# A transformer block in fp32: another order of work in the attention loop, at its beginning and end, and ScalarE issuing the last V stores of the first stage

## The chip, the cores and the metric

One core of a Trainium2 chip runs the whole kernel in one launch. The metric is the device time in microseconds. Three runs of the kernel before took 1292.84, 1295.64 and 1298.81 us; the median is 1295.64 us. The engines are TensorE (PE in the profile; PEld are its weight loads), VectorE (DVE), ScalarE (ACT), GpSimd (POOL) and SyncE (SP), which issues DMAs.

## The reference

The input `x` is 32 sequences of 100 rows with 320 features; the context has 361 rows of 192 features for each sequence. There are 20 heads of 16 features.

```
def _attn(x, ctx, wq, wk, wv, wo, bo, heads):
    q, k, v = x @ wq, ctx @ wk, ctx @ wv          # each split into heads
    sim = einsum('bhid,bhjd->bhij', q, k) * dh ** (-0.5)
    out = einsum('bhij,bhjd->bhid', softmax(sim, axis=-1), v)
    return out (heads joined) @ wo + bo
h1 = _ln(x, n1_g, n1_b)
x = _attn(h1, h1, q1, k1, v1, o1_w, o1_b, heads) + x
h2 = _ln(x, n2_g, n2_b)
x = _attn(h2, context, q2, k2, v2, o2_w, o2_b, heads) + x
h3 = _ln(x, n3_g, n3_b)
a, g = split(h3 @ ff_w1 + ff_b1, 2, axis=-1)
return (a * gelu(g)) @ ff_w2 + ff_b2 + x
```

## The kernel before

The program has three stages, each a block of its own in which every engine runs a list of instructions written out by hand; a block begins when all engines have left the one before it. Engines wait for each other by semaphores.

The first stage normalises `x` and computes queries, keys and values of the first ("own") attention for all 32 sequences, four at a time (eight groups `k`). ScalarE copies each sequence's values out of PSUM into `v_rows` (`copy_values`, L2295), and SP stores queries and keys (`qk_dram`, L1905) and values (`store_values`, L1860) to HBM.

The second stage is the attention phase. It works on one sequence in each of four roles at a time: in period `p` of the loop (`PERIODS`, 29 of them) `x = p` is in its second ("cross") attention, `s = p + 1` has its cross scores' maxima taken, `c = p + 2` is in its own attention and gets its cross queries and keys, and `f = p + 3` has its own maxima taken. `lead_in` fills this pipeline and `run_out` drains it. Each engine has its own `lead_in`, `period` and `run_out`, in which the calls stand in the order in which the engine does them. The names of the steps on TensorE: `self_scores(f, i)` (L168) is one half of the own scores, whose maximum VectorE takes (L175); `cross_scores(s, i)` (L786) is a pair of heads of the cross scores, ten calls for a sequence, each followed by VectorE's maximum (L1096) before the next may overwrite PSUM; `scores_for_exp(a, b, g, jt)` (L812) computes the scores again with the maximum in an extra row, for ScalarE's exponential (L1419), a = 1 for own, 2 for cross; there are two PSUM banks for it and 11 buffers for the exponentials. `times_v(a, b, g)` (L834) multiplies them with the values. `project_kc` (KC, L733 to L737) and `project_vc` (VC, L748 to L752) make cross keys and values from the context, `project_q2` and `turn_q2` (Q2, QT) the cross queries, `turn_max` (MT1, MT2; L797) turns the maxima, `turn_normalised` (T2) the normalised rows, `project_out` (O1, O2; L703, L706) is the output projection. These projections share three PSUM banks in turn, in the order of the lists `FILL_WORK`, `work_jobs` and `DRAIN_WORK`; a job waits for the bank of the job three before it.

SP moves operands between the steps. `load_qkv1(b)` brings the own queries, keys and values ("own stack", L86 to L103, nine loads); its first use of a stored sequence waits for all stores of the first stage. `load_context(b)` brings a context (L145, L146) as soon as GpSimd has split the one before it into high and low parts (`split_first`, `split_last`, L1656, L1657). `place_kc`, `place_q2` and `place_max` copy keys (L550), queries (L568) and maxima (L160) into the stacks that the scores read; `place_q2` waits until GpSimd has cleared the stack (`clear_cross`), `load_qkv1` likewise for `clear_own` (both L1610). SP works in order, so a step that waits holds up everything behind it.

The third stage is the feed-forward part, in five passes of 640 rows.

Of the kernel before, what the change touches and what calls it, by code (L numbers as in the profile page):

```python
# [31 lines left out]
NB = 4  # L32
# [12 lines left out]
def work_jobs(x, s, c, f):  # L45
    y = None if x is None or x == 0 else x - 1
    order = [("MT2", x, 0), ("VC", s, 2), ("O2", y, 0), ("MT1", f, 0), ("KC", c, 0), ("KC", c, 1), ("O1", c, 0),
             ("T2", c, 0), ("KC", c, 2), ("Q2", c, 0), ("QT", c, 0), ("VC", c, 0), ("VC", c, 1)]
    return [job for job in order if job[1] is not None]
# [8 lines left out]
def exp_jobs(x, s, c, f):  # L58
    order = [(1, c, 1, 0), (1, c, 2, 0), (1, c, 3, 0), (1, c, 4, 0), (2, x, 0, 0), (2, x, 0, 1), (2, x, 0, 2),
             (2, x, 1, 0), (2, x, 1, 1), (2, x, 1, 2), (2, x, 2, 0), (2, x, 2, 1), (2, x, 2, 2), (2, x, 3, 0),  # L60
             (2, x, 3, 1), (2, x, 3, 2), (2, x, 4, 0), (2, x, 4, 1), (2, x, 4, 2), (1, f, 0, 0)]
# [142 lines left out]
def over(jobs):  # L204
# [4 lines left out]
FILL_WORK = [("O1", 0, 0), ("VC", 0, 0), ("VC", 0, 1), ("MT1", 1, 0), ("T2", 0, 0), ("KC", 0, 0), ("KC", 0, 1),  # L209
             ("Q2", 0, 0), ("QT", 0, 0), ("VC", 0, 2), ("KC", 0, 2), ("KC", 1, 0), ("MT1", 2, 0), ("O1", 1, 0),  # L210
             ("KC", 1, 1), ("T2", 1, 0), ("Q2", 1, 0), ("QT", 1, 0), ("VC", 1, 0), ("VC", 1, 1), ("KC", 1, 2)]
FILL_SCORE = [(1, 1, 0), (1, 1, 1), (1, 2, 0), (1, 2, 1), (2, 0, 0), (2, 0, 1), (2, 0, 2), (2, 0, 3), (2, 0, 4),
              (2, 0, 5), (2, 0, 6), (2, 0, 7), (2, 0, 8), (2, 0, 9)]
FILL_EXP = [(1, 1, 0, 0), (1, 1, 1, 0), (1, 1, 2, 0), (1, 1, 3, 0), (1, 1, 4, 0), (1, 2, 0, 0)]
FILL_PV = [(1, 1, 0), (1, 1, 1), (1, 1, 2), (1, 1, 3), (1, 1, 4)]
DRAIN_WORK = [("MT2", 29, 0), ("VC", 30, 2), ("O2", 28, 0), ("KC", 31, 0), ("O1", 31, 0), ("KC", 31, 1),
              ("T2", 31, 0), ("Q2", 31, 0), ("QT", 31, 0), ("KC", 31, 2), ("MT2", 30, 0), ("VC", 31, 0),
              ("VC", 31, 1), ("VC", 31, 2), ("MT2", 31, 0), ("O2", 29, 0), ("O2", 30, 0), ("O2", 31, 0)]
# [3 lines left out]
DRAIN_EXP = [(1, 31, 1, 0), (1, 31, 2, 0), (1, 31, 3, 0), (1, 31, 4, 0), (2, 29, 0, 0), (2, 29, 0, 1), (2, 29, 0, 2),  # L222
# [2648 lines left out]
```

## Time and profile before

| what | us |
|---|---|
| median of three runs | 1295.64 |
| lowest and highest | 1292.84, 1298.81 |
| the profiled execution, its own time | 1297.57 |
| its span, first to last instruction | 1295.8 |
| TensorE busy | 1228.0 (95%) |
| VectorE, ScalarE, GpSimd busy | 828.9, 671.4, 601.5 |

The profile is of one execution. TensorE's weight loads (PEld) run beside its products. A row of a timeline gives the start, the length, the engine, the source line, the operation with its output and inputs, and in brackets how long the engine had been idle and what released it. A row may hold several instructions (x4); for SP the length is that of issuing, not of the transfer. The first stage takes the first 150 us, the attention phase lasts until about 935 us, the rest is the feed-forward part. The granted clock of TensorE is given as a share of 2.4 GHz.

### The profile page before, as it was taken

The page shows a single profiled execution, that of the slowest core. Times are in us where ns is not written, and L with a number is a line of the kernel's source. Part 1 is how long each engine was busy: PE and PEld are TensorE (multiplying, and loading weights), DVE is VectorE, ACT ScalarE, POOL GpSimd, SP SyncE. Part 2 cuts the span into 40 slices and gives each one's busy share as a digit, 9 for nine tenths or more (in the row PEclk, how much of TensorE's full clock was granted, in tenths as well). Part 3 has the DMA queues.
Part 4 walks back from the last instruction along what each step waited for, and adds up shares of the span by engine and source line. Part 5 has one row for each costly group of instructions (what it writes and reads, how often), then busy time and mean ns, then how long its engine had stood idle before and what let it go on. Part 6 is the DMA issues. An engine that isn't in the chain of part 4 may idle for free. (4 is left out here: it accounts for less than half of the span.)

```text
span 1295.8 us, 34279 instructions
## 1 busy us (share of the span) xinstructions
PE 1228.0 (95%) x12788; PEld 1135.1 (88%) x12788; DVE 828.9 (64%) x1606; ACT 671.4 (52%) x1622; POOL 601.5 (46%) x792
## 2 busy tenths in 40 slices
PE   6899769999999999999999999998799999999999
PEld 4899758888888888888888888886699999999999
DVE  5454447888888888888888888876565243332521
ACT  5565326666666666666666666664552322323131
POOL 5431125546555465555655546551564443423331
PEclk9999859999999999999999999999899999999999
DMA  4576645454555655556454554533021101010000
GB/s 128 192 236 215 217 124 157 133 175 130 150 158 160 187 153 176 158 165 186 132 168 135 148 166 134 164 110 98 26 60 37 36 11 41 0 51 0 25 1 26
DMA packets 105145, 154.49 MB, mean 119 GB/s; under 512 B 20780, under 2 KB 86564, under 8 KB 104996
## 3 DMA queue, kind: packets, MB, share of 16 engines
q1 hardware_dynamic: 104996, 152.49, 38.6%
q8 instruction: 95, 1.56, 0.5%
q14 instruction: 54, 0.44, 0.1%
HBM read 62.98 MB, written 28.93 MB: 71 GB/s over the span
## 5 line engine op out<-in xcount | busy, mean ns | idle before, releaser
L1419 ACT ACTIVATE probs<-expin 120x400 f32<-120x400 f32 (+2 forms) x635 | 297.5, 506 | 129.7 <-PE expin L812 126.0
L1096 DVE TENSOR_REDUCE neg_max<-score 100x2 f32<-100x722 f32 x320 | 288.0, 900 | 94.4 <-PE score L786 92.9
L812 PE MATMUL expin<-qs,ks 128*120 128x200 f32 (+2 forms) x1270 | 201.4, 272 | 3.8 <-DMA qs<-max_parts 1.8
L812 PEld LDWEIGHTS expin<-qs,ks 128*120 128x120 f32 (+2 forms) x1270 | 178.3, 181 | 16.3 <-ACT probs L1419 8.1
L786 PE MATMUL score<-ks,qs 128*100 128x362 f32 x640 | 170.5, 348 | 18.9 <-DVE neg_max L175 10.6
L2658 DVE SCALAR_TENSOR_TENSOR hidden<-ps_a,b_cols,gelu 128x320 f32<-128x320 f32 x100 | 55.1, 551 | 165.5 <-PE ps_a L2582 165.5
L2820 POOL TENSOR_TENSOR hid_lo<-hidden,hid_hi 128x320 fp32r<-128x320 f32 x100 | 88.1, 881 | 122.0 <-ACT hid_hi L2728 121.8
L1610 POOL MEMSET qs<- 128x2400 f32 (+1 forms) x58 | 112.6, 1941 | 69.0 <-PE expin L812 69.0
L2740 ACT ACTIVATE gelu<-ps_g,b_cols 128x320 f32<-128x320 f32 x100 | 52.7, 527 | 137.1 <-PE ps_g L2582 137.1
L786 PEld LDWEIGHTS score<-ks,qs 128*100 128x100 f32 x640 | 87.3, 168 | 40.5 <-issue 29.7
L834 PE MATMUL attn<-probs,vc 120*17 120x100 f32 (+1 forms) x3840 | 109.2, 253 | 0.0
L191 POOL TENSOR_TENSOR scaled_heads<-turned_heads,rden 128x320 f32<-128x320 f32 x63 | 47.9, 760 | 130.9 <-DVE rden L196 130.9
L834 PEld LDWEIGHTS attn<-probs,vc 120*17 120x17 f32 (+1 forms) x3840 | 78.7, 98 | 18.4 <-issue 8.5
L2582 PE MATMUL ps_g<-t_hi,w_hi 128*128 128x320 f32 x300 | 92.3, 313 | 2.4 <-DVEq L2497 2.4
L2582 PE MATMUL ps_g<-t_hi,w_lo 128*128 128x320 f32 x300 | 91.6, 310 | 0.0
L2582 PE MATMUL ps_a<-t_hi,w_lo 128*128 128x320 f32 x300 | 91.4, 310 | 0.0
L2582 PE MATMUL ps_a<-t_hi,w_hi 128*128 128x320 f32 x300 | 91.4, 310 | 0.0
L175 DVE TENSOR_REDUCE neg_max<-score 100x10 f32<-100x1000 f32 x62 | 74.3, 1199 | 15.2 <-PE score L168 13.5
L2599 PE MATMUL ps_y<-w_hi,hid_hi 128*128 128x320 f32 x250 | 78.5, 314 | 0.0
L2600 PE MATMUL ps_y<-w_lo,hid_hi 128*128 128x320 f32 x250 | 77.1, 308 | 0.0
L2601 PE MATMUL ps_y<-w_hi,hid_lo 128*128 128x320 f32 x250 | 77.1, 308 | 0.0
L1951 PE MATMUL qk_ps<-ks,w_qkv 128*128 128x400 f32 x320 | 70.5, 364 | 1.1 <-issue 1.1
(222 smaller groups left out, 2899.4 us busy)
## 6 DMA issues: line engine op xcount, KB each, us to landing
ks<-kc_parts SPq DMA_DIRECT2D x96, 362.0 KB, 3.7
qk_dram<-qk_parts SPq DMA_DIRECT2D x32, 500.0 KB, 5.4
qs<-q_parts SPq DMA_DIRECT2D x192, 75.0 KB
ks<-qk_dram SPq DMA_DIRECT2D x96, 125.0 KB
ctx_raw<-in_ctxT SPq DMA_DIRECT2D x64, 180.5 KB
ks<-kc_parts SPq DMA_DIRECT2D x96, 90.5 KB, 2.7
qs<-qk_dram SPq DMA_DIRECT2D x64, 125.0 KB
v_dram<-v_rows SPq DMA_DIRECT2D x32, 132.8 KB
```

What stands on the lines that cost most here:

```text
L175: return nc.vector.tensor_reduce(neg_max[:, :, n * i:n * (i + 1)], src, AX_X, ALU.max, negate=True)
L786: mm = pe.matmul(score[0:N, a, 0:JP], qs[2][u][:, a, q_slot(c), :], ks[2][u][:, k_slot(c), :], start=True, stop=True)
L812: mm = pe.matmul(dst, ks[a][u][:, k_slot(c) if a == 2 else c, j0:j0 + n], qs[a][u][:, :, q_slot(c) if a == 2 else c, :], start=True, stop= ...
L834: mm = pe.matmul(attn[32 * i:32 * i + D1, g * N:(g + 1) * N], v, probs[EXP_AT[a, b, g, jt] % NPT][0:n, i * N:(i + 1) * N], start=(jt == 0) ...
L1096: ins = nc.vector.tensor_reduce(dst, src, AX_X, ALU.max, negate=True)
L1419: nc.scalar.activation(probs[e % NPT][0:n, :], expin[e % 2][0:n, 0:HG * N], ACT.Exp, scale=SCALE)\
L1610: link(nc.gpsimd.memset(stack.rearrange("p a c n -> p (a c n)").bitcast(F32), 0.0))
L2582: mm = pe.matmul(bank[:, 0:W], a, b, start=(k == 0), stop=(k == len(passes) - 1))
L2599: pe.matmul(y, hid_hi[:, f, c], w2_hi[:, f, :], start=(f == 0), stop=False)
L2600: pe.matmul(y, hid_hi[:, f, c], w2_lo[:, f, :], start=False, stop=False)
L2601: mm = pe.matmul(y, hid_lo[:, f, c], w2_hi[:, f, :], start=False, stop=(f == FT - 1))
L2820: nc.gpsimd.tensor_tensor(hid_lo[:, f, c], hidden[n % 2][:], hid_hi[:, f, c].bitcast(F32), ALU.subtract).then_inc(hid_lo_made, 1)
```

## The change

Nothing that is computed changes. There are three parts. The lists that assign PSUM banks follow the order of the calls (in `work_jobs`, for one, `("KC", c, 2)` now stands ahead of `("T2", c, 0)`, and in `exp_jobs` `(1, c, 0, 0)` comes first and `(1, f, 0, 0)` is gone from the end). Line numbers of the changed kernel are one or two off those of before.

First, the last group's four V stores of the first stage are issued by ScalarE, each behind the next copy, and no longer by SP:

```
-                else:
+                elif k < NK - 1:
                     store_values(k)
...
+            def store_last(i):
+                b = (NK - 1) * NB + i
+                act.wait_ge(v_made, b + 1)
+                act.dma_start(v1_dram[b], v_rows[i][:].rearrange("p h d -> p (h d)")).then_inc(v_stored[i], 16)
...
                 copy_values((NK - 1) * NB + i)
                 if i == 2:
                     heads_high()
+                if i:
+                    store_last(i - 1)
+            store_last(NB - 1)
```

On ScalarE, at the end of the first stage, `v_rows0` to `v_rows3` being the last four sequences' values, there stood

```order
L2295 COPY v_rows0<-v1_pair 100x20x16
L2295 COPY v_rows1<-v1_pair 100x20x16
L2295 COPY v_rows2<-v1_pair 100x20x16
L2310 CAST t_hi_OT<-dense_heads_87 128x300
L2295 COPY v_rows3<-v1_pair 100x20x16
```

and now

```order
L2293 COPY v_rows0<-v1_pair 100x20x16
L2293 COPY v_rows1<-v1_pair 100x20x16
L2299 DMA v1_dram<-v_rows0 100x340
L2293 COPY v_rows2<-v1_pair 100x20x16
L2313 CAST t_hi_OT<-dense_heads_87 128x300
L2299 DMA v1_dram<-v_rows1 100x340
L2293 COPY v_rows3<-v1_pair 100x20x16
L2299 DMA v1_dram<-v_rows2 100x340
L2299 DMA v1_dram<-v_rows3 100x340
```

A store stands behind the copies of the next sequence's values, and the last two stores are the stage's last instructions there.

Second, the beginning and the end of the attention phase have a new order on all engines. SP's beginning:

```
             def lead_in():
-                load_qkv1(2)
                 set_key_rows()
-                place_max(1, 1)
                 load_context(1)
+                load_x(1)
+                load_qkv1(2)
+                place_max(1, 1)
                 place_kc(0, 0)
                 place_q2(0)
-                load_x(1)
+                load_context(2)
+                place_kc(0, 2)
+                load_x(2)
                 load_qkv1(3)
                 place_max(1, 2)
-                load_x(2)
-                place_kc(0, 2)
-                load_context(2)
+                load_x(3)
                 place_kc(1, 0)
-                load_x(3)
```

On SP the phase began, the own stack being `qs_0`, `ks_0` and `vs` from `qk_dram` and `v_dram`, with

```order
L86 DMA qs_0_74<-zeros 2x20x100
L96 DMA ks_0_76<-qk_dram 32x1000 x3
L100 DMA qs_0_74<-qk_dram 32x1x1000
L102 DMA qs_0_74<-qk_dram 16x1000
L100 DMA qs_0_74<-qk_dram 32x1x1000
L102 DMA qs_0_74<-qk_dram 16x1000
L103 DMA vs_78<-v_dram 100x340
L606 DMA ks_0<-pv 2x10x362
L606 DMA ks_1<-pv 2x10x362
L160 DMA qs_1_75<-max_parts 1x20x100 x2
L145 DMA ctx_raw<-in_ctxT 128x361
L146 DMA ctx_raw<-in_ctxT 128x1x361
```

and now, behind the two rows for the constant key rows (`ks_0<-pv`, `ks_1<-pv`), with

```order
L145 DMA ctx_raw<-in_ctxT 128x361
L146 DMA ctx_raw<-in_ctxT 128x1x361
L509 DMA xin<-in_x 100x320
L86 DMA qs_0_74<-zeros 2x20x100
L96 DMA ks_0_76<-qk_dram 32x1000 x3
L100 DMA qs_0_74<-qk_dram 32x1x1000
L102 DMA qs_0_74<-qk_dram 16x1000
L100 DMA qs_0_74<-qk_dram 32x1x1000
L102 DMA qs_0_74<-qk_dram 16x1000
L103 DMA vs_78<-v_dram 100x340
L160 DMA qs_1_75<-max_parts 1x20x100 x2
L551 DMA ks_0<-kc_parts 32x4x724 x3
```

Context and residual input stand ahead of the own stack, the maxima directly behind it. On TensorE `project_kc(1, 0)` stood between the own products and the first cross scores; there `project_vc(0, 2)` stands now, and `project_kc(1, 0)` follows the first cross scores. On VectorE `second_input(0)` and `statistics(0)` come before the first own maximum. At the end, TensorE has `project_vc(30, 2)` and `cross_scores(30, 0)` ahead of `project_out(2, 28)` rather than `cross_scores` behind it, `turn_tile(1)` behind the last `times_v`, and VectorE has `result(29)` ahead of the last `turn_heads`.

Third, the loop. The first exponent step of a sequence, `(1, f, 0, 0)`, leaves the end of a period and stands as `(1, c, 0, 0)` at the beginning of the next; the same in ScalarE's list. TensorE's and SP's periods:

```
                 self_scores(f, 0)
+                scores_for_exp(1, c, 0, 0)
+                turn_max(2, x)
                 scores_for_exp(1, c, 1, 0)
+                project_vc(s, 2)
                 scores_for_exp(1, c, 2, 0)
-                turn_max(2, x)
-                project_vc(s, 2)
                 scores_for_exp(1, c, 3, 0)
+                self_scores(f, 1)
                 scores_for_exp(1, c, 4, 0)
-                self_scores(f, 1)
...
                 cross_scores(s, 4)
-                times_v(2, x, 0)
+                project_kc(c, 2)
                 scores_for_exp(2, x, 2, 2)
                 scores_for_exp(2, x, 3, 0)
-                times_v(2, x, 1)
+                times_v(2, x, 0)
...
                 turn_normalised(c)
-                project_kc(c, 2)
+                times_v(2, x, 1)
...
                 cross_scores(s, 8)
-                scores_for_exp(1, f, 0, 0)
                 times_v(2, x, 3)
...
                 load_context(f)
                 place_kc(s, 2)
+                load_qkv1(e)
                 load_x(e)
+                place_kc(c, 0)
+                store_x2(y)
                 place_max(1, f)
-                load_qkv1(e)
-                store_x2(v)
-                place_kc(c, 0)
```

On TensorE, in front of the first cross scores of a period (the row with `qs2_0`; `vs1` are own values, `expin` the exponents' banks), there stood

```order
L812 MATMUL expin0<-qs1_1_75,ks1_1_77 100x200 x2
L812 MATMUL expin1<-qs1_1_75,ks1_1_77 100x200 x2
L168 MATMUL score<-ks1_0_76,qs1_0_74 100x100 x10
L834 MATMUL attn<-probs9,vs1_79 17x100 x4
L834 MATMUL attn<-probs10,vs1_79 17x100 x4
L834 MATMUL attn<-probs0_80,vs1_79 17x100 x4
L834 MATMUL attn<-probs1_81,vs1_79 17x100 x4
L834 MATMUL attn<-probs2_82,vs1_79 17x100 x4
L786 MATMUL score<-ks2_0,qs2_0 100x362 x2
```

and now

```order
L811 MATMUL expin1<-qs1_1_75,ks1_1_77 100x200 x2
L811 MATMUL expin0<-qs1_1_75,ks1_1_77 100x200 x2
L168 MATMUL score<-ks1_0_76,qs1_0_74 100x100 x10
L811 MATMUL expin1<-qs1_1_75,ks1_1_77 100x200 x2
L833 MATMUL attn<-probs9,vs1_79 17x100 x4
L833 MATMUL attn<-probs10,vs1_79 17x100 x4
L833 MATMUL attn<-probs0_80,vs1_79 17x100 x4
L833 MATMUL attn<-probs1_81,vs1_79 17x100 x4
L833 MATMUL attn<-probs2_82,vs1_79 17x100 x4
L785 MATMUL score<-ks2_0,qs2_0 100x362 x2
```

One more exponent step stands between the second own scores (L168) and the cross scores. It comes from the end of the period, where there stood

```order
L786 MATMUL score<-ks2_1,qs2_1 100x362 x2
L812 MATMUL expin1<-qs1_1_75,ks1_1_77 100x200 x2
L834 MATMUL attn<-probs3_83,vc0 17x100 x4
L834 MATMUL attn<-probs4_84,vc0 17x100 x4
L834 MATMUL attn<-probs5,vc0 17x100 x4
L834 MATMUL attn<-probs6,vc0 17x100 x4
L834 MATMUL attn<-probs7,vc0 17x100 x4
L834 MATMUL attn<-probs8,vc0 17x100 x4
L786 MATMUL score<-ks2_1,qs2_1 100x362 x2
```

and now

```order
L785 MATMUL score<-ks2_1,qs2_1 100x362 x2
L833 MATMUL attn<-probs3_83,vc0 17x100 x4
L833 MATMUL attn<-probs4_84,vc0 17x100 x4
L833 MATMUL attn<-probs5,vc0 17x100 x4
L833 MATMUL attn<-probs6,vc0 17x100 x4
L833 MATMUL attn<-probs7,vc0 17x100 x4
L833 MATMUL attn<-probs8,vc0 17x100 x4
L785 MATMUL score<-ks2_1,qs2_1 100x362 x2
```

ScalarE copies `copy_vc(c, 0)` at the end of the period rather than at the beginning of the next. GpSimd does `first_residual(f)` first in a period rather than `first_residual(e)` near its end, and `clear_cross(c)` before `second_residual(c)`. VectorE's period is the same.

## Rows read from the trace of the kernel before

**Rows 1.** busy time of each engine, granted clock and DMA in three stretches

```profile
145.00:150.00 5.00, 0.00 (x0) 0.00 (x0) 0.81 (x1) 0.42 (x1) 2.35 (x2) 0.75 0.96 346
...
165.00:170.00 5.00, 4.02 (x21) 3.13 (x21) 1.39 (x2) 1.66 (x5) 0.00 (x0) 0.50 0.74 236
...
600.00:650.00 50.00, 49.19 (x653) 44.38 (x652) 42.13 (x74) 32.78 (x82) 27.18 (x31) 1.00 0.51 151
```

**Rows 2.** timeline of TensorE; columns: start us, length us, engine, line, operation, [idle before, releaser]

```profile
150.42 1.08 PE L168 MATMUL score<-ks,qs 64*100 64x100 f32 x10 [5.46 <-PEq L1769]
...
163.28 0.64 PE L168 MATMUL score<-ks,qs 64*100 64x100 f32 x10 [2.80 <-DMA vs<-v_dram]
...
166.37 0.99 PE L812 MATMUL expin<-qs,ks 128*100 128x200 f32 x4 [0.98 <-DMA qs<-max_parts]
...
171.05 1.87 PE L834 MATMUL attn<-probs,vs 100*17 100x100 f32 x40
...
177.29 0.64 PE L733 MATMUL work<-ctx_hi,w_c 128*128 128x362 f32 x1 [4.37 <-POOL ctx_lo L1657]
...
179.00 0.91 PE L786 MATMUL score<-ks,qs 128*100 128x362 f32 x2
...
180.92 0.92 PE L786 MATMUL score<-ks,qs 128*100 128x362 f32 x2 [1.00 <-DVE neg_max L1096]
...
198.83 0.64 PE L168 MATMUL score<-ks,qs 64*100 64x100 f32 x10 [0.27 <-DVE neg_max L1096]
```

**Rows 3.** timeline of SP's queue around the phase's beginning (issue times)

```profile
145.84 4.02 SPq L1860 DMA_DIRECT2D v_dram<-v_rows  x4
...
154.96 0.59 SPq L86 DMA_DIRECT2D qs<-zeros  x1
...
160.74 0.51 SPq L103 DMA_DIRECT2D vs<-v_dram  x1
...
162.50 2.17 SPq L160 DMA_DIRECT2D qs<-max_parts  x2
```

**Rows 4.** timelines of ScalarE and GpSimd, last work of the first stage

```profile
145.00 0.42 ACT L2295 COPY v_rows<-v_pair 100x320 f32<-100x320 f32 x1 [0.41 <-PE v_pair L1981]
...
145.56 1.86 POOL L2423 TENSOR_TENSOR ctx_lo<-ctx_raw,ctx_hi 128x724 fp32r<-128x724 f32 x1
```

**Rows 5.** timeline of TensorE, one period of the loop

```profile
503.11 0.54 PE L786 MATMUL score<-ks,qs 128*100 128x362 f32 x2 [0.41 <-DVE neg_max L175]
...
518.36 0.34 PE L812 MATMUL expin<-qs,ks 128*100 128x200 f32 x2
...
518.63 0.61 PE L834 MATMUL attn<-probs,vc 120*17 120x100 f32 x18
```

**Rows 6.** waits in the loop, 222 to 870 us: total us, times, longest us

```profile
PE score L786 <- DVE neg_max L175: 10.2, 25, 0.4
...
PE score L786 <- DMA qs<-q_parts: 1.7, 3, 0.7
```

**Rows 7.** timelines of SP's queue and GpSimd, one period of the loop

```profile
507.70 0.52 SPq L508 DMA_DIRECT2D xin<-in_x  x1
...
515.76 1.92 SPq L550 DMA_DIRECT2D ks<-kc_parts  x3
...
519.57 4.09 SPq L568 DMA_DIRECT2D qs<-q_parts  x6
...
506.44 1.77 POOL L1610 MEMSET qs<- 128x2000 f32 x1
```

**Rows 8.** timelines of TensorE and VectorE, end of the attention phase

```profile
871.72 0.95 PE L703 MATMUL work<-w_o,t_hi_OT 128*100 128x320 f32 x5 [0.71 <-ACT t_hi_OT L1440]
...
918.95 0.90 PE L853 MATMUL score<-identf,h 128*128 128x128 f32 x3 [1.00 <-DVE h L1209]
...
932.48 1.05 PE L706 MATMUL work<-w_o,t_lo_OT 128*100 128x320 f32 x3
...
934.26 0.49 DVE L1158 TENSOR_TENSOR x<-work,xres 100x320 f32<-100x320 f32 x1 [1.66 <-DMA x_dram<-x]
```

More of the change, by code:

```diff
@@ L648, in period @@
                 y = x - 1 if x else None
-                v = y - 1 if y else None
                 place_q2(s)
@@ L1011, in run_out @@
                 times_v(2, 31, 4)
+                turn_tile(1)
                 turn_tile(2)
@@ L1262, in run_out @@
                 turn_back(1, 31)
+                result(28)
                 maximum(2, 30, 1)
                 kc_low(31, 0)
-                result(28)
                 second_input(31)
@@ L1284, in run_out @@
                 maximum(2, 31, 1)
+                maximum(2, 31, 2)
+                kc_low(31, 2)
+                maximum(2, 31, 3)
                 turn_back(2, 29)
-                maximum(2, 31, 2)
-                maximum(2, 31, 3)
                 maximum(2, 31, 4)
@@ L1297, in run_out @@
                 tile_statistics(1)
+                turn_heads(2, 30)
                 normalise_tile(1)
-                turn_heads(2, 30)
+                turn_back(2, 30)
                 tile_statistics(2)
-                turn_back(2, 30)
+                tile_low(0)
                 normalise_tile(2)
-                tile_low(0)
-                tile_low(1)
+                result(29)
                 turn_heads(2, 31)
                 turn_back(2, 31)
+                tile_low(1)
+                result(30)
                 tile_low(2)
-                result(29)
-                result(30)
                 result(31)
@@ L1469, in lead_in @@
                 copy_q2(1)
-                exponential(1, 2, 0, 0)
                 q2_high(1)
@@ L1474, in run_out @@
             def run_out():
-                copy_vc(30, 0)
+                exponential(1, 31, 0, 0)
                 exponential(1, 31, 1, 0)
+                max_high(2, 29)
                 exponential(1, 31, 2, 0)
-                max_high(2, 29)
                 exponential(1, 31, 3, 0)
                 exponential(1, 31, 4, 0)
+                heads_high(2, 28)
+                copy_vc(30, 1)
+                copy_product(1, 31)
                 copy_vc(30, 2)
-                copy_vc(30, 1)
-                heads_high(2, 28)
-                copy_product(1, 31)
                 exponential(2, 29, 0, 0)
@@ L1504, in run_out @@
                 q2_high(31)
+                exponential(2, 29, 4, 2)
+                copy_vc(31, 0)
+                copy_product(2, 29)
+                copy_vc(31, 1)
+                max_high(2, 30)
                 kc_high(31, 2)
-                exponential(2, 29, 4, 2)
-                copy_product(2, 29)
-                max_high(2, 30)
                 exponential(2, 30, 0, 0)
@@ L1554, in period @@
                 copy_vc(s, 1)
-                copy_vc(s, 0)
+                exponential(1, c, 0, 0)
                 exponential(1, c, 1, 0)
+                max_high(2, x)
                 exponential(1, c, 2, 0)
-                max_high(2, x)
                 exponential(1, c, 3, 0)
@@ L1585, in period @@
                 exponential(2, x, 4, 2)
-                exponential(1, f, 0, 0)
                 q2_high(c)
                 copy_product(2, x)
+                copy_vc(c, 0)
             lead_in()
```

171 lines of the change are left out of this document (83 added, 88 removed), and 13 rows, old and new, of the table DRAIN_EXP.

## The prediction

> **What bounds the kernel now.** I read the busy time by stretches first, then TensorE's timeline where a stretch is weak, then the queue or engine that its gap names. In the loop TensorE is busy for 49.19 of 50 us at clock 1.00; between 165 and 170 it is busy for 4.02 of 5 us at 0.50, which is the level of 1.2 GHz [rows 1]. So there are three places. The beginning: between the last product of the first stage and the loop's first period at 198.83 TensorE has gaps of 5.46, 2.80, 0.98 and 4.37 us [rows 2]. The loop: one gap of 0.41 us a period, in front of the first cross scores, for the second own maximum [rows 5, 6]. The end: a few gaps of about 1 us and a last addition that waits for a store [rows 8]. The feed-forward part behind it is untouched and carried over at its length.
>
> **The end of the first stage.** SP issues the last four V stores from 145.84 to 149.86 [rows 3], and TensorE's 5.46 us end at 150.42 [rows 2], 0.56 us behind them: the stage's barrier waits for SP. Without these four, SP is free at 145.84. GpSimd then ends at 147.42 and ScalarE copies its last rows until 145.42 [rows 4]. No row shows a DMA issued by ScalarE. The nearest are SP's: 0.51 us for the V load, and 4.02/4 = 1.0 us for these stores [rows 3]. Two stores come behind the last copy, and the two ahead of it delay that copy by at most 1 us: ScalarE ends between 146.5 and 148.4. Below nothing is excluded only as long as an issue stays under about 1.5 us. I take 1.0 us, since it is the same transfer, and less the part that falls into gaps: the barrier at about 148.0 and TensorE's start at 148.5, 1.9 us sooner.
>
> **The loop's beginning.** Before, SP's first issue of the phase waits until 154.96 for the stores to land, 5.1 us behind the last of them; the own stack takes until 161.25, and the maximum's rows are out at 164.67 [rows 3]. TensorE's own scores start 2.0 us behind the stack's last issue, and the exponents 1.7 us behind the maximum's [rows 2]. Now the constant key rows, context 1 and x 1 go first. The key rows took 1.2 us (161.25 to 162.50) [rows 3]; five issues at some 0.6 us make about 3 us, in which SP waited before (148 to 151), and the own loads follow when the stores have landed. With their last issue at about 147.5 to 148.4 that is 152.6 to 153.5; I take 152.6, as the first three stores are out by 147. The stack's issue (6.3 us) ends at 158.9, the maximum's (2.2 us) at 161.1, and the exponents can start at 162.8 rather than 166.37. TensorE is there in time: before, it was done with its list at 160.48 (163.28 - 2.80); the list now starts 1.9 us sooner, has a wait of about 1.5 us in it, since VectorE does the statistics before the first maximum, and turns q2 first, about 0.9 us with ScalarE's copy (both estimates). That gives 161.0 for the next own scores, just where their stack lands (158.9 + 2.0). So 3.5 us are won here. From the exponents to the end of the own products is 6.55 us (166.37 to 172.92) and stays so: 169.4. Then the 4.37 us go: KC(1,0) waited for context 1, whose load stood behind own stack and maximum; now that load is out by 151 and GpSimd's split waits for VC(0,1) and VC(0,2) alone. VC(0,2), five products at the 0.3 us that those of KC(1,0) take at this clock (177.29 to 179.00 for five and a turn), comes first, and the first cross scores start at 171.0, not 179.00. What is late next is the q2 stack: it follows the maximum and the keys on SP and lands at about 168 to 170, so 1 to 3 us in front of its use. KC(1,0), 1.7 us, now lies between the first two cross scores, where TensorE waited 1.00 us for the maximum anyway [rows 2]: 0.7 us more. The loop starts at 198.83 - 8.0 + 0.7 = 191.5, **7.3 us sooner**. Bounds: 4 us, if the stores land no sooner and the new waits are twice as long; 11 us, if TensorE, with shorter gaps, does not fall to clock 0.50.
>
> On the stores, rows 1 show the DMA engines 96% busy from 145 to 150 us. The Trainium skill, "DMA: Bandwidth & Descriptors", section "Issuing engines are not separate DMA queues", speaks against this part: all issuing engines use the same 16 DMA engines, and a second one only saves issue time. By that rule the stores would land at 154.9 as before, and only what stood between them and the exponents is won; the rival below prices that from rows.
>
> **The loop.** Order matters here only where TensorE waits. Its gap ends with VectorE's second own maximum, a fixed time behind the second own scores, and the own products alone do not fill that time [rows 5]. The change moves one pair of exponent products, 0.27 us long (518.36 to 518.63), from the end of a period to its beginning and so one pair into this gap: 0.41 becomes about 0.14, and the place that it left closes up. The wait occurs in 25 rows of 28 periods, and in the other three the q2 stack is late [rows 6]. Does something else become late? The pair's ScalarE work moves with it, and the V copy that it meets has moved to the period before; the last exponential is done just before its product wants it. KC(c,2) moves forward by three crosses, over a bank and a split that are ready; T2 comes 0.25 us later against its normalised input, which is slack. Matmul pairs change neighbours at some eight places a period; such a change costs or saves up to 0.1 us, which I cannot sign. SP: before, x, maximum, own loads, store and keys take 10.0 us in a row (507.70 to 517.68), and the next q2 stack starts at 519.57 [rows 7]: 1.9 us free. Now the same list begins with the own loads, which cannot start before GpSimd has cleared their stack (508.21): it ends at 518.3, and the q2 stack is due 0.27 sooner, at 519.3. One microsecond is free, so nothing waits. 28 x 0.27 = 7.6 us; I take **7.5**. Bounds: 0 (the q2 stack takes the place of the maximum) to 11 (the whole 0.41).
>
> **The end.** VC(30,2) and the first cross scores now stand ahead of O2(28), which covers its 0.71 us, and the second turned tile, in front of which TensorE waited 1.00 us, goes behind the last products [rows 8]. VectorE adds result 29 before the last heads, so the last addition no longer waits for that store: it started at 934.26, O2(31) ends at 933.53, so 0.7 us. Together **2.4 us**. Two turned maxima get other work ahead of them as well, but ScalarE's exponentials stand close behind; I set these against each other. Bounds: a loss of 2, if the new order makes as many gaps as it closes, and a gain of 6.
>
> **Sum.** The profiled execution took 1297.57 us (span 1295.8): 1297.6 - 7.3 - 7.5 - 2.4 = 1280.4. The median of the runs lies 1.9 us below that execution, so **1278.5 us**; the rivals are given on that scale.
>
> **Rivals.**
> 1. The stores land no sooner. Own loads from 154.96 to 161.25, the maximum's rows directly behind them, out at 163.4, exponents at 165.1: 1.3 us are won there instead of 3.6, and the 4.4 us of KC(1,0) stay won. 1281. For it: the 96% of rows 1. Against: the wait for the stores is 5.1 us behind an issue that lay 4 us later than needed. 0.15.
> 2. In the loop the gap stays: the pair goes in, but the q2 stack ends last, as in three periods already. No gain there: 1286. Against: its trigger, GpSimd's clearing behind the last exponent pair, keeps its distance. 0.15.
> 3. The clock holds: with no gap over 2 us behind 161 us, TensorE keeps 1.00, and what it did at half of that until the loop is limited by VectorE's maxima alone: 3 to 4 us more: 1275. Against: one gap of 2.80 us was enough to lose it. 0.15.
> 4. Slower: SP's list does not fit. The maximum's rows now go out last, just ahead of the q2 stack, so whatever the own loads take too long delays both, and through them the first exponents and cross scores of every period. It decides from the free 1.0 us on: the own loads alone took 6.3 us at the beginning, so a sixth more for them uses it up. At 2.1 us more a period, each is 1.1 us later than forecast: 28 x 1.1 = 31 us, 1309. 0.05.
> 5. The new end loses as much as the beginning wins, through ScalarE: 1288. 0.05.
>
> The forecast has 0.45, between 1273 and 1284. What a measurement of this kernel tells from no change is about 0.5%, 6.5 us: faster is below 1289.2. All cases but the fourth and parts of 2 and 5 lie there: 0.84 faster, 0.11 the same, 0.05 slower. Range for eight in ten: 1269 to 1290.
>
> **What would show it.** First product of the phase at about 148.5; no wait of KC(1,0) for the split; first cross scores near 171 and the loop's first own scores near 191.6; the period 22.76 us rather than 23.03, its gap 0.1 to 0.2 us; the last addition without a wait for a store. Wrong, if the gap in front of the cross scores is put down to the q2 stack in most periods, if new gaps stand in front of exponents, or if the phase does not start before 150.

## The result: half a per cent faster, a third of the forecast

The changed kernel takes 1289.83 us (median of 20 runs, 1284.9 to 1297.4), the kernel before on the same chip 1295.57 (20 runs): a ratio of 0.995, 95% interval 0.9936 to 0.9964, so some 6 us where 17 were forecast. On a second chip the ratio was 0.9973 (0.9957 to 0.999).

Two executions of the kernel before and three of the changed one were profiled (those behind the first pair come from the experiments below). Stages in us, each from the timeline of TensorE (start of a row, less the wait in its brackets where the end of the work before is meant; the loop's 28 periods are counted from 0, and its 29th, the last, belongs to the end):

| Stage | before | before, second | forecast | after | after, second | after, third |
|---|---|---|---|---|---|---|
| last product of the first stage to the loop's start | 53.9 | 53.0 | 46.5 | 46.5 | 47.0 | 44.3 |
| the loop's first period | 23.0 | 23.0 | 22.8 | 24.5 | 23.7 | 27.5 |
| its other 27 periods | 623.4 | 622.6 | 615.9 | 621.5 | 625.2 | 626.7 |
| start of the 29th period to the feed-forward part | 90.7 | 89.7 | 88.3 | 86.7 | 86.4 | 89.8 |
| feed-forward part | 359.9 | 360.7 | 359.9 | 360.1 | 360.4 | 359.7 |

The beginning won what was forecast and the end no less. The loop, from which 7.5 us were to come, gives nothing: with its first period it took 646.0, 648.8 and 654.1 us, before 646.4 and 645.6. The first period alone is 0.6 to 4.4 us longer than before.

First the three stretches of [rows 1] in the changed kernel (columns: stretch, length, busy us of PE, PEld, DVE, ACT, POOL with counts, granted clock, DMA share, GB/s):

```profile
145.00:150.00 5.00, 2.07 (x19) 2.04 (x20) 1.52 (x6) 0.32 (x1) 2.80 (x5) 0.98 0.96 316
165.00:170.00 5.00, 5.00 (x28) 4.40 (x28) 1.73 (x2) 1.63 (x4) 0.59 (x1) 0.50 0.51 174
600.00:650.00 50.00, 49.23 (x663) 44.07 (x659) 40.16 (x70) 32.66 (x84) 26.00 (x29) 1.00 0.51 160
```

TensorE starts 2.5 us sooner, and the DMA engines are as full as before. TensorE's timeline at the beginning, against [rows 2]:

```profile
147.93 0.64 PE L168 MATMUL score<-ks,qs 64*100 64x100 f32 x10 [3.07 <-PEq L1767]
...
164.43 1.07 PE L168 MATMUL score<-ks,qs 64*100 64x100 f32 x10 [2.82 <-DMA vs<-v_dram]
...
167.00 0.87 PE L811 MATMUL expin<-qs,ks 128*100 128x200 f32 x4
...
172.80 0.55 PE L785 MATMUL score<-ks,qs 128*100 128x362 f32 x2
174.59 0.41 PE L732 MATMUL work<-ctx_hi,w_c 128*128 128x362 f32 x1 [1.24 <-POOL ctx_lo L1656]
...
191.36 0.64 PE L168 MATMUL score<-ks,qs 64*100 64x100 f32 x10 [0.26 <-DVE neg_max L1095]
```

SP's queue beside it, against [rows 3], and ScalarE's, which had no DMA in [rows 4]:

```profile
154.38 0.54 SPq L86 DMA_DIRECT2D qs<-zeros  x1
...
159.32 0.51 SPq L103 DMA_DIRECT2D vs<-v_dram  x1
159.88 1.67 SPq L160 DMA_DIRECT2D qs<-max_parts  x2
```

```profile
142.56 0.63 ACTq L2299 DMA_DIRECT2D v_dram<-v_rows  x1
...
143.73 0.28 ACTq L2299 DMA_DIRECT2D v_dram<-v_rows  x1
...
144.90 2.48 ACTq L2299 DMA_DIRECT2D v_dram<-v_rows  x2
```

The own loads still begin at 154.38, their stack lands 4.6 us behind its last issue (159.83 to 164.43) instead of 2.0, and the first exponents start at 167.00, not at 162.8. But the 4.37 us for context 1 are down to 1.24, and TensorE's granted clock is back at 1.00 from 170 us instead of 188 (it falls once more, until 180 here and until 195 before). The loop starts at 191.36 (forecast 191.5).

In the loop the wait of [rows 6] for the second own maximum is gone. A period in which nothing waits takes 22.76 to 22.85 us, as forecast. What came instead, in the waits of TensorE's matmuls and weight loads over periods 1 to 27 (total us, times, longest):

```profile
PE expin L811 <- DMA qs<-max_parts: 2.7, 6, 0.9
PE score L785 <- DMA qs<-q_parts: 0.6, 2, 0.4
PE expin L811 <- ACT probs L1418: 0.5, 1, 0.5
```

```profile
PEld expin L811 <- DMA qs<-max_parts: 5.2, 11, 1.1
```

These are rows of maxima that SP places in the stacks, seven times the own maximum's (3.4 us) and four times the cross maximum's (1.9 us). Two periods of the changed kernel side by side, first without and then with such a wait, TensorE and then SP:

```profile
330.02 0.64 PE L168 MATMUL score<-ks,qs 64*100 64x100 f32 x10
330.60 0.43 PE L811 MATMUL expin<-qs,ks 128*100 128x200 f32 x2
...
398.47 0.64 PE L168 MATMUL score<-ks,qs 64*100 64x100 f32 x10
400.05 0.43 PE L811 MATMUL expin<-qs,ks 128*100 128x200 f32 x2 [0.94 <-DMA qs<-max_parts]
```

```profile
325.66 1.66 SPq L160 DMA_DIRECT2D qs<-max_parts  x2
...
393.88 1.90 SPq L160 DMA_DIRECT2D qs<-max_parts  x2
```

The issue ends 2.70 us (327.32) and 2.69 us (395.78) ahead of the period: no difference. The first exponents follow 0.6 us into the period, so the rows have 3.3 us to land. In the one case that was enough, in the other they took 4.3. Over all periods both numbers vary: the issue ends 1.5 to 4.1 us ahead of the period where nothing waits and 1.3 to 2.8 ahead where TensorE does, and there the rows land 2.1 to 4.3 us behind it.

The lists of the two cases differ in one thing. Ahead of the late rows SP had also brought weights of the feed-forward part (`load_w1`, 256 and 128 KB), which it does in periods 8 to 17 only:

```profile
380.12 0.51 SPq L643 DMA_DIRECT2D w_raw<-in_ff_w  x1
380.68 0.62 SPq L644 DMA_DIRECT2D w_raw<-in_ff_w  x1
```

### The profile page after: what moved, and what is told of

It reads as the page before. It is cut to its first block and busy times, and to the rows that moved or that the text cites. A ratio compares the mean times of both kernels' runs of the same rounds, so it can differ in the third digit from the quotient of the medians.

```text
span 1284.1 us, 34279 instructions
## 1 busy us (share of the span) xinstructions
PE 1224.0 (95%) x12788; PEld 1127.6 (88%) x12788; DVE 814.2 (63%) x1606; ACT 668.2 (52%) x1622; POOL 601.2 (47%) x792
## 5 line engine op out<-in xcount | busy, mean ns | idle before, releaser
L1418 ACT ACTIVATE probs<-expin 120x400 f32<-120x400 f32 (+2 forms) x635 | 293.3, 505 | 132.3 <-PE expin L811 130.3
L811 PE MATMUL expin<-qs,ks 128*120 128x200 f32 (+2 forms) x1270 | 197.0, 272 | 6.3 <-ACT probs L1418 3.0
L785 PEld LDWEIGHTS score<-ks,qs 128*100 128x100 f32 x640 | 83.6, 166 | 38.4 <-issue 21.0
L1636 POOL TENSOR_TENSOR t_lo_OT<-dense_heads,t_hi_OT 128x300 fp32r<-128x300 f32 x63 | 52.6, 835 | 49.1 <-ACT t_hi_OT L1439 42.9
```

The source lines that it names most:

```text
L785: mm = pe.matmul(score[0:N, a, 0:JP], qs[2][u][:, a, q_slot(c), :], ks[2][u][:, k_slot(c), :], start=True, stop=True)
L811: mm = pe.matmul(dst, ks[a][u][:, k_slot(c) if a == 2 else c, j0:j0 + n], qs[a][u][:, :, q_slot(c) if a == 2 else c, :], start=True, stop= ...
L1418: nc.scalar.activation(probs[e % NPT][0:n, :], expin[e % 2][0:n, 0:HG * N], ACT.Exp, scale=SCALE)\
```

## Experiments

**Less waiting ahead of SP's list.**

```
-                load_context(f)
                 place_kc(s, 2)
+                load_context(f)
                 load_qkv1(e)
```

> The changed kernel with one line moved on SP: in the loop's period the third key tile (place_kc(s, 2)) goes ahead of the context load, where SP waits up to 2.6 us for GpSimd's split. Theory A (SP's list is full, so its last entries, the own maximum's rows and with them the q2 stack and the cross maximum's rows, are late by chance in 11 places, 5.2 us): the list gets 0.9 to 2.6 us of room in each period, the waits for maximum rows in the loop fall below 1 us in total, periods 1 to 27 take 22.8 us each (615 to 617 us together instead of 621.5), about 5 us faster than the changed kernel: some 1285 us against the kernel before at 1295.6. Rival B (the rows land late because the DMA engines are busy, wherever they are issued): waits stay, 1290. Rival C (the context, now 0 to 1 us later, becomes the wait): waits for ctx_lo appear on TensorE, 1290 or more.

Measured: 1297.0 us against 1297.4, ratio 0.9995 (0.9976 to 1.0014). Theories A and C fell; the waits stayed, as in rival B, but the time lies above its 1290. No wait for the context came, but the list did not become shorter either, as SP's wait only moved to GpSimd's clearing of the own stack (0.4 us in the changed kernel), and the waits for maximum rows were longer:

```profile
SPq L532 <- POOLq L1610: 43.0, 27, 3.1
```

```profile
PEld expin L811 <- DMA qs<-max_parts: 12.1, 13, 1.8
```

One of them shows what a wait can cost. The period from 401.09 takes 27.30 us, 4.5 more than a clean one, for a wait of 1.63:

```profile
403.36 0.43 PE L811 MATMUL expin<-qs,ks 128*100 128x200 f32 x2 [1.63 <-DMA qs<-max_parts]
```

```profile
404.00:406.00 2.00, 2.00 (x18) 1.82 (x19) 0.67 (x2) 1.70 (x5) 0.80 (x1) 0.69 0.02 7
406.00:408.00 2.00, 2.00 (x36) 1.73 (x38) 1.20 (x1) 0.96 (x4) 0.00 (x0) 0.50 0.09 13
408.00:410.00 2.00, 2.00 (x24) 1.66 (x17) 0.28 (x1) 0.94 (x3) 1.88 (x3) 0.50 0.68 187
410.00:412.00 2.00, 2.00 (x10) 1.88 (x10) 1.66 (x3) 0.11 (x1) 0.43 (x2) 0.61 0.70 165
412.00:414.00 2.00, 2.00 (x17) 2.00 (x16) 1.73 (x3) 1.53 (x5) 2.00 (x2) 1.00 0.17 60
```

Behind the wait the granted clock (third number from the end) is at 0.50, the level of 1.2 GHz, for some seven microseconds (404.7 to 411.6).

**The own maximum's rows back ahead of the own loads.**

```
                 place_kc(s, 2)
+                place_max(1, f)
                 load_qkv1(e)
                 load_x(e)
                 place_kc(c, 0)
                 store_x2(y)
-                place_max(1, f)
```

> The changed kernel with one call moved on SP: the own maximum's rows (place_max(1, f)) go out ahead of the own loads, where they stood before the change; the list keeps its length. Theory A (length decides): of the waits in front of exponents the seven for own maximum rows (3.4 us) go, the four for cross maximum rows (1.9 us) stay, since q2 stack and cross maximum are as late as now: 1286 to 1287 us. Theory A2 (the place of the own rows alone decides): all eleven go, 1285. Rival B (landing, not issue): no change, 1290. Rival D: the own loads, 1.7 us later, are late for the next own scores: waits for vs in front of the own scores, 1290 or slower.

Measured: 1288.2 us, ratio 0.9929 (0.9909 to 0.995), 6 us faster than the changed kernel on the same chip. Loop 643.8 us; the own rows' waits are gone, the cross rows' remain, as theory A has it, and the q2 stack is late in five places:

```profile
PEld expin L811 <- DMA qs<-max_parts: 1.5, 5, 0.4
```

```profile
PE score L785 <- DMA qs<-q_parts: 3.3, 5, 1.2
```

**SP's beginning in the old order.**

```
-                set_key_rows()
-                load_context(1)
-                load_x(1)
                 load_qkv1(2)
+                set_key_rows()
                 place_max(1, 1)
+                load_context(1)
+                load_x(1)
```

> The changed kernel with SP's lead-in begun as before the change: own stacks, key rows, maximum rows, and only then context 1 and x 1; all other orders stay new. Theory A (context ahead of the own loads is what wins at the beginning, although the own stack landed 4.6 us behind its last issue): the stack lands some 2 us sooner (about 162.4 us), but KC(1,0) waits for a context that lands some 12 us later, 2 to 4 us lost by the loop's start (193.5 to 195.5 instead of 191.4): 1292 to 1294 us. Rival B (the order of these loads has no weight, because the stores' landing at 154.4 and the DMA engines' share set everything behind): loop start within 1 us of 191.4, 1290. Rival C (the context's transfers in front cost more than they give): loop start sooner, 1287.

Measured: 1298.0 us, ratio 0.9999 (0.9982 to 1.0016), 3.7 us slower than the changed kernel beside it (the two intervals just overlap). Theory A holds in size: the loop starts 50.5 us behind the last product of the first stage instead of 44.3 to 47.0. The own stack lands 2.2 us behind its issue. What waits then is not the context, though, but the q2 stack behind it:

```profile
163.28 1.07 PE L168 MATMUL score<-ks,qs 64*100 64x100 f32 x10 [1.50 <-DMA vs<-v_dram]
...
179.08 0.90 PE L785 MATMUL score<-ks,qs 128*100 128x362 f32 x2 [6.94 <-DMA qs<-q_parts]
```

**The changed kernel again** (no edit).

> The changed kernel unaltered, as the measure for the other three on the same chip, with a second profile. If the 12 us between the two profiled executions are the change, this profile starts its loop near 191.4 and its feed-forward part near 924 as the first did, and the time is 1286; if part of it was one execution's clock, one of the two is later, with more rows at clock 0.50, and the median stays at 1290.

Measured: 1294.4 us, ratio 0.9973 (0.9957 to 0.999). Beginning and end came out as in the first profile, but the loop was 2.8 us longer, with ten waits for own rows instead of seven, 6.7 us:

```profile
PEld expin L811 <- DMA qs<-max_parts: 8.5, 15, 1.5
```

**Two small entries more out of SP's list.** On top of the second experiment:

```
+                load_x(e)
                 load_context(f)
                 place_kc(s, 2)
+                store_x2(y)
                 place_max(1, f)
                 load_qkv1(e)
-                load_x(e)
                 place_kc(c, 0)
-                store_x2(y)
```

> The kernel of the second experiment (own maximum's rows ahead of the own loads), and in the loop's period on SP two small entries more moved out of the list behind GpSimd's clearing: the x load ahead of the context load, the x2 store ahead of the maximum's rows. Its profile had a loop of 643.8 us, 6.0 over 28 periods of 22.78, with 3.3 us of waits for the q2 stack and 1.5 for cross maximum rows. Theory A (what stands on SP between GpSimd's clearing of the own stack and the q2 stack is too long by chance, up to 1.2 us): the list gets 0.9 to 1.4 us shorter there, waits for q2 and maximum rows fall below 1.5 us together, loop 639 to 641 us, 3 us less than that kernel. Rival B (the stacks land late because of the traffic, not of the issue): loop 643 to 646, same time as that kernel. Rival C (the store in front delays the own loads): waits for vs in front of own scores, slower.

Measured: 1285.7 us, ratio 0.9897 (0.9873 to 0.992), the best kernel here. It is 2.5 us faster than the second experiment by the medians, 4 by the ratios, which fits theory A, but its profile does not: its loop took 646.2 us instead of 639 to 641. SP had the room (it waits 21.4 us for GpSimd's clearing instead of 7.8), yet the q2 stack was late as often, 3.2 us in five places. In the longest, 1.6 us, its issue ended 2.9 us into the period (586.07 for a period from 583.15) where clean ones have 2.2; the other 0.9 us are its landing. So rival B is right for a good part of these waits. The intervals of this kernel and the second one overlap, so which of the two is faster is not settled.

**Exponents ahead of the own scores at the beginning.** On top of the fifth, on TensorE:

```
                 turn_q2(0)
-                self_scores(2, 0)
                 project_kc(0, 2)
                 scores_for_exp(1, 1, 0, 0)
                 scores_for_exp(1, 1, 1, 0)
+                self_scores(2, 0)
```

> The kernel of the fifth experiment, with one call moved in TensorE's lead-in: the own scores of item 2 go behind KC(0,2) and the first two pairs of exponent products, so that TensorE does not wait for item 2's own stack (2.05 to 5.98 us in four profiles) with work in hand. Theory A (that stack is what is late, while the maximum's rows of item 1 are issued 1.7 us behind it and needed only by the exponents): KC(0,2) and two pairs, some 3 us at half clock, fill the wait; the loop starts 2 to 3 us earlier than in the fifth experiment, about 189.5. Rival B (the maximum's rows land no sooner than the stack): the wait only moves in front of the first exponents, loop start within 0.7 us of the fifth's, no gain. Rival C (item 2's own maxima become late for its turned maximum): a new wait for VectorE, up to 1 us lost.

Measured: 1287.0 us, ratio 0.992 (0.9897 to 0.9943). The wait for the stack is gone and no other came, but the loop starts 47.8 us behind the first stage, not sooner. The work that fills the wait runs at half clock, and so does what follows:

```profile
165.00:170.00 5.00, 4.95 (x28) 3.92 (x26) 1.72 (x3) 1.55 (x4) 0.51 (x1) 0.50 0.60 213
170.00:175.00 5.00, 5.00 (x59) 4.28 (x60) 2.02 (x2) 2.12 (x6) 1.69 (x2) 0.50 0.05 17
```

In the fifth experiment the second of these stretches has 1.00, but the tenth, with TensorE's order of the fifth, has 0.50 there too:

```profile
170.00:175.00 5.00, 5.00 (x60) 4.24 (x60) 1.73 (x2) 2.17 (x7) 2.20 (x2) 0.50 0.28 89
```

So the clock can fall there with either order, and these single profiles do not show that the moved work is the reason. The theories left the clock out.

**ScalarE's stores alone**, in the kernel before:

```
-                else:
+                elif k < NK - 1:
                     store_values(k)
...
+                if i:
+                    store_last(i - 1)
+            store_last(NB - 1)
```

> The kernel before the change, with only the last four V stores moved from SP to ScalarE. Theory A (the barrier waits for SP's issues, but the stores' landing is set by the DMA engines, 96 to 100% busy there): the phase starts 2 to 2.5 us sooner, at 148, the own loads still begin at 154 to 155.5, TensorE waits that much longer for the own stack, the loop starts where it did (198.3 to 199.3): 1295 to 1297, no difference. Rival B (the forecast: the stores land sooner by as much as they are issued sooner): own loads at 152.6, loop start 196.5 to 197, 2 us faster.

Measured: 1299.5 us against 1297.5, ratio 1.0007 (0.9991 to 1.0023): nothing. The phase starts 2.94 us behind the first stage's last product instead of 5.46, but the own loads begin 9.95 us behind it (147.31), as before (10.0). In its profile the loop starts 51.6 us behind that product, 1.4 to 2.3 sooner than before, but its first period takes 24.5 us instead of 23.0.

```profile
150.25 1.07 PE L168 MATMUL score<-ks,qs 64*100 64x100 f32 x10 [2.94 <-PEq L1769]
```

```profile
157.26 0.59 SPq L86 DMA_DIRECT2D qs<-zeros  x1
```

**The old end**, on top of the second experiment (first lines of TensorE's):

```
                 scores_for_exp(1, 31, 0, 0)
-                turn_max(2, 29)
                 scores_for_exp(1, 31, 1, 0)
+                turn_max(2, 29)
                 scores_for_exp(1, 31, 2, 0)
+                project_vc(30, 2)
```

> The kernel of the second experiment with the last periods' order of before the change on all engines (the pair of exponent products that the loop no longer does put at its head). Theory A (the new order of the end is worth what two profiles of it show: 86.2 to 86.7 us from the last loop period to the feed-forward part, against 90.7 before): it takes 90 to 91 us again, 4 us slower than the second experiment, 1292 or 0.997 of the kernel before. Rival B (most of these 4 us are a clock that happened to hold): 86 to 88 us, no difference to the second experiment. Rival C (only the forecast's 2.4 us): 88.6 to 89.

Measured: 1291.1 us, ratio 0.9949 (0.9931 to 0.9967), 2.6 us slower than the second experiment by the two ratios, near rival C; the two were measured on different chips and their intervals overlap, so the time alone does not settle it. Its end took 92.6 us at a mean clock of 0.94, 2.3 of them in one wait for keys. Here are the changed kernel's first and third profile and the kernel before in its second, over the same stage:

```profile
837.38:924.05 86.67, 73.39 (x944) 60.89 (x944) 60.78 (x109) 48.77 (x120) 39.34 (x51) 0.98 0.27 74
```

```profile
843.41:933.21 89.80, 76.44 (x945) 63.73 (x944) 60.76 (x109) 48.81 (x120) 39.37 (x51) 0.94 0.25 71
```

```profile
844.85:934.53 89.68, 74.61 (x942) 62.39 (x942) 61.41 (x109) 48.50 (x120) 39.65 (x51) 0.95 0.25 72
```

The last two, at nearly the same clock, show no difference. But the clock varies, and so do single profiles; here are the eighth and the tenth experiment (old and new end), both at 0.94:

```profile
838.54:931.16 92.62, 76.08 (x945) 63.76 (x944) 60.95 (x109) 48.50 (x120) 39.75 (x51) 0.94 0.26 71
```

```profile
839.65:927.19 87.54, 76.39 (x944) 63.88 (x944) 60.78 (x109) 48.80 (x120) 39.35 (x51) 0.94 0.26 74
```

Over all profiles, TensorE is idle in this stage (length less the first busy time) for 11.0 to 13.4 us in the ten with the new end, and for 14.2 to 16.5 us in the four with the old one (the two of the kernel before, the seventh and the eighth experiment). Where the mean clock is between 0.90 and 0.95, the new end takes 87.5 to 90.7 us (five profiles) and the old one 89.7 to 92.6 (four).

**Maximum's rows last, but sooner.** On top of the changed kernel:

```
+                load_x(e)
                 load_context(f)
                 place_kc(s, 2)
+                store_x2(y)
                 load_qkv1(e)
-                load_x(e)
                 place_kc(c, 0)
-                store_x2(y)
                 place_max(1, f)
```

> The changed kernel with the x load ahead of the context load and the x2 store behind the third key tile, as in the fifth experiment, but the own maximum's rows still last on SP, behind the own loads and keys. In the changed kernel their last issue ends 2.7 us before the next period in periods with a wait and without one alike, and they land 3.8 to 5.3 us behind it where there is a wait, so 0.3 to 1.6 us late. Theory A (they are due too soon behind their issue; only that room counts): they are issued 1 to 2 us sooner, the waits of the first own exponents (7 to 10 a run, 3.4 us and more) fall below 1 us in total, and the time comes within 2 us of the fifth experiment, 0.991 of the kernel before. Rival B (landing behind the keys' 362 KB in the same queue holds them, wherever the list ends): these waits stay above 2.5 us, 0.995 or more.

Measured: 1288.5 us, ratio 0.9927 (0.9904 to 0.9951). Of the waits for own rows four are left, 1.3 us; with the cross rows':

```profile
PEld expin L811 <- DMA qs<-max_parts: 3.5, 9, 0.6
```

A little over the 1 us of theory A and, in this one profile, below rival B's 2.5. The rows were issued 0.6 us sooner in the mean, still behind the keys: the room between issue and use counts, even in this place.

**x 1 behind the q2 stack at the beginning**, on top of the fifth:

```
                 load_context(1)
-                load_x(1)
                 load_qkv1(2)
                 place_max(1, 1)
                 place_kc(0, 0)
                 place_q2(0)
+                load_x(1)
```

> The kernel of the fifth experiment with the load of x 1 moved in SP's lead-in from ahead of the own loads to behind the q2 stack. Theory A (traffic in front on the same queue is why item 2's own stack landed 4.0 to 4.7 us behind its last issue, and 2.0 to 2.2 us where own loads went first): with only the keys and the context in front it lands 3 to 4 us behind it, the wait for vs is about 1 us shorter, and the loop starts up to 1 us sooner after the end of the first stage's products (46 us instead of 47). Rival B (the landing is set by something else, such as the stores still under way): 4.0 us or more again, nothing gained. Rival C (x 1 comes late for its residual): a new wait at project_out's addition, later loop.

Measured: 1285.7 us, ratio 0.9902 (0.9881 to 0.9924). The stack landed 3.8 us behind its issue (161.89 to 165.66), the loop started 47.0 us behind the first stage: no gain. The landing lies in theory A's range, the loop's start is as in rival B. What holds the stack back remains open between the context's transfer and the stores.

**Third profile of the changed kernel, second of the one before** (no edits).

> The changed kernel unaltered, for a third profile of its loop. So far its loop took 646.0 and 648.8 us, and 650.7 with the old beginning; that before took 646.4 and 649.7. Theory A (the loop's term of the forecast, 7.5 us, is nearly all given back by waits for stacks): 645 to 651. Theory B (those profiles were unlucky): 640 to 643.

> The kernel before unaltered, for a third profile of its loop, its end and its beginning. Theory A: loop 645 to 650 us, the loop's start 51.5 to 54 us behind the last product of the first stage, the end 90 to 92.5 us from the last loop period to the feed-forward part. Theory B (the profiled execution of before was an unlucky one in its end): end 87 to 88.

Measured: one run each, 1294.6 and 1297.0 us; the stages stand in the table. The loop of the changed kernel took 654.1 us, with 10.2 us of waits for rows in its later 27 periods; that of before 645.6:

```profile
PEld expin L811 <- DMA qs<-max_parts: 10.2, 14, 1.5
```

The loop of the changed kernel lies 3 us above theory A's range, most of it in its first period of 27.5 us, where TensorE waits for the q2 stack:

```profile
195.97 0.90 PE L785 MATMUL score<-ks,qs 128*100 128x362 f32 x2 [2.34 <-DMA qs<-q_parts]
```

For the kernel before theory A held, its end of 89.7 us leaving 90 by a little.

## Why the prediction was wrong

**The step that failed** is in the part on the loop, on SP's list: "it ends at 518.3, and the q2 stack is due 0.27 sooner, at 519.3. One microsecond is free, so nothing waits." That priced the issue of the list against the issue of the next stack. It did not price the landing of the list's last entry, and the loop's term, 7.5 us, came out at nothing. The own maximum's rows moved to the list's end while their first use moved with the pair of exponents to 0.6 us into the next period: some 3 us from issue to use, where before 8.4 us lay between, from the end of this issue to 518.36 in [rows 5]:

```profile
508.37 1.64 SPq L160 DMA_DIRECT2D qs<-max_parts  x2
```

At the beginning, with the DMA engines 30% busy from 160 to 165 us, TensorE had them 1.7 us behind their issue [rows 2, 3]. In the loop they took 2.1 to 4.5 us where it waited (three profiles), and the issue itself ended 0.6 to 3.3 us ahead of the next period, 2.2 in the mean, where the forecast's 518.3 had left 3.2. One of the prediction's own signs of being wrong came true: new gaps in front of exponents. The change is shown to be the cause: with the rows back ahead of the own loads their waits went from 7, 10 and 11 in three profiles to none, and 6 us came back in the time.

Nor was a microsecond free. SP's wait for GpSimd's clearing in front of the next q2 stack is the time that its list leaves over; over the 27 periods it shrank from the first of these rows (before) to the second (changed), to 0.3 us a period, and there was none in 11 of them:

```profile
SPq L562 <- POOLq L1611: 32.5, 26, 2.0
```

```profile
SPq L563 <- POOLq L1610: 8.1, 16, 1.0
```

What the rows land behind shows in the traces' semaphore events, which tell when a transfer is complete: in 68 of 81 periods of the three profiles they land 0.7 to 1.05 us behind the last of the three key transfers that go out just ahead of them. These take 4.0 us each from issue to landing, by the page of the changed kernel:

```profile
ks<-kc_parts SPq DMA_DIRECT2D x96, 362.0 KB, 4.0
```

The Trainium skill, "DMA: Bandwidth & Descriptors", section "Queues, rings and completion order", says that a transfer's semaphore increment lands only after every earlier write of the same DMA engine. By that rule a small transfer behind a large one lands no sooner than the large one, and these distances agree with it. No run puts the rows last without the keys in front.

The weights of the feed-forward part seem to add to it, and neither the prediction nor an experiment looks at them. Rows issued in the periods with `load_w1` land 3.2 us behind their issue in the mean (30 periods of the three profiles), in the others 2.1 (51), with the same room, and 19 of the 28 waits follow them. The kernel before has the same difference, 5.5 against 3.6 us, but 8.4 us of room. No run moves these loads, so their part is not shown.

**The fourth rival** had the place (rows last on SP, first exponents and cross maxima late) but only lateness of issue for its mechanism, 2.1 us in every period, and a chance of 0.05. What happens is issue and landing together, late by 0.2 to 1.5 us in a quarter to two fifths of the periods: 6 to 12 us over 27 clean periods, enough for the loop's whole term, and not 31.

**The loop's gain** is there in every clean period, some 22.8 us against 23.03. With the own rows placed sooner the 27 periods took 619.7 to 623.0 us in five profiles (second, fifth, sixth, eighth and tenth experiment), 621.1 in the mean, against 624.4 in the changed kernel's three; 27 clean ones would be 615. So the place of the own rows accounts for 3 us in the profiles and not for all that the loop missed. What stays is mostly the q2 stack and the cross maximum's rows, late too; that the 0.4 us which VectorE's maximum cost in each period had been their margin as well is my reading, not shown.

**ScalarE's stores**: the phase's start at 148.5 was right (147.9), its worth was not. The first rival's condition holds: the own loads, which wait for the first stage's stores, can start no sooner. The Trainium skill, in the same page's section "Issuing engines are not separate DMA queues", says that a second issuing engine saves only issue time. The seventh experiment agrees, with 9.95 us against 10.0.

**The beginning** was right in its sum (7.5 us in the mean of the profiles, 7.3 forecast) by luck, for its parts were wrong: the exponents were 4.2 us late, and KC(1,0) still waited 1.24 us. What made it up is, as far as the rows show, the clock, which returned 18 us sooner in the first profile. The third rival had a part of that, and some of it goes again: in two of three profiles the clock falls in the loop's first period, behind waits of 0.28 and 0.92 us in the first of them and of 2.34 us in the third, and that period takes 1.7 and 4.7 us more than a clean one. The forecast had no wait for the q2 stack there. That key rows, context 1 and x 1 ahead of the own loads are worth some 3.5 us is shown by the third experiment.

**The end** was right, in its gaps too. In the first profile of the changed kernel O2(28) and the second turned tile start without a wait, and the last addition no longer waits for the store of [rows 8]:

```profile
922.41 0.49 DVE L1157 TENSOR_TENSOR x<-work,xres 100x320 f32<-100x320 f32 x1 [0.72 <-issue]
```

New gaps came too: one of 1.44 us stands in front of the first cross scores there. TensorE's idle time in the stage is below that with the old order in every profile (eighth experiment). In time it is 2.6 us by the eighth experiment against 2.4 forecast, but the intervals overlap.

## What to carry to other kernels

When a use moves forward and its load moves back, price the distance from the load's issue to its use in the busy part of the kernel, not where the queue is empty, and ask what goes out ahead of it in the same queue. A wait that bounds a loop by a little may also be the margin of everything that ends just before it: price the next two that end there by their spread, not by their mean. Do not count a stage's gaps alone where the clock moves: the same order, with 13.3 and 13.4 us of gaps, took 86.7 and 89.8 us.

## What the runs showed of the chip

- A wait of 1.63 us in a loop with TensorE otherwise busy was followed by seven microseconds at clock 0.50 and cost 4.5 us in all; one of 0.94 us cost 1.0, with the clock at 1.00 throughout. Over the 20 runs of the changed kernel the mean granted clock goes from 0.978 (1297.4 us) to 0.988 (1284.9 us). How much of that spread comes from such waits no run isolates; the kernel before spreads by 9 us as well.
- Two transfers of 7.8 KB each, put out in a busy queue behind three of 362 KB, landed 1.3 to 4.5 us behind their issue (81 periods, three profiles of one kernel).
- DMAs issued by ScalarE took it 0.63, 0.28 and twice 1.24 us; the copies between them kept their pace.
